# Attention kernel with two passes per head: projections and output products gathered in one gap of the unit, the first block's weighing moved to the next gap

## Chip, core and metric

One core of a Trainium2 chip runs the kernel. The metric is the device time of one execution in microseconds, the median of several. Before the change it is 2521.51 us, the median of three runs between 2519.04 and 2525.44.

## The reference, cut to what matters

The input `x` is 32 x 512 tokens x 256 channels (16 heads of 16). For each of the 32 batches:

```
qk = x @ W_attn + b_attn ; q, k = halves of qk ; v = x          (heads of 16 channels)
y  = causal_softmax(q k^T / 4) v
e  = v[1:] - y[:-1] ; k2 = x[:-1] @ W_k2 + b_k2 ; q2 = q[1:]
y2 = causal_softmax(q2 k2^T / 4) e, shifted by one token (first row zero)
x  = layernorm(x + (y + y2) @ W_proj + 2 b_proj)
```

Then a mixture of 8 experts (top 2) is added and a second layernorm follows. The routing table has 512 rows, so that the experts add to batch 0 alone; for the other batches the kernel folds the two layernorms into one.

## The kernel before

The program is unrolled by hand over a clock of slots. A **unit** is one attention pass over one group of four heads of one batch. There are 8 units in a batch: places 0 to 3 are the first attention, places 4 to 7 the second. A unit has ten slots, and every engine's program is written in the same order of slots. "(3, 6)" is slot 6 of place 3. The letters below are used in the whole text.

TensorE (PE) fills in each slot a PSUM bank of transposed scores (`score_t`, L651) of the present unit for the exponentials, and beside it, in the other half of the array's rows, a bank of plain scores (`score`, L662) of the unit five units ahead, for the row maxima. There are three banks of each kind. These products are gathered in four **runs**: R0 (slots 0, 1, 2), R3 (slots 3, 4), R5 (slots 5, 6, 7) and R8 (slots 8, 9). All other work of PE lies in the four gaps behind the runs:

- gap 1, behind R0: **W123**, the weighing of key blocks 1, 3 and 2 of the previous unit (`weigh`, L612), which adds into `out_t`. At places 3 and 7 a transpose of the maxima follows, **N** (L717).
- gap 2, behind R3: **H** (L677), four transposes of `heads_t`, which ScalarE has copied from `out_t` (L536). At places 1 and 2, **Y** follows (L730), four transposes of `y_sum`. It waits for the last additions into `y_sum` on GpSimd (L476).
- gap 3, behind R5: half a projected tile, three matmuls (**P**, L703), or a quarter of the output projection (**J**, L744), then **W0**, the weighing of block 0, which opens `out_t` anew (L758).
- gap 4, behind R8: the other half of the P tile, or the next quarter of J.

Six places of a batch (7, 0, 1, 2, 4, 5) have a P tile, for the batch ahead; places 3 and 6 have J. P, J, N and Y all write the one PSUM bank `misc`.

ScalarE (ACT) takes an exponential of each `score_t` bank in order of slots (L518). When a P tile is complete it copies `misc` to `part_f` (L528); at (0, 7), (0, 9), (1, 1), (1, 3) it applies the first layernorm to a finished batch (L275), the first time after waiting for `shift` (L263) from GpSimd.

VectorE (DVE) takes the row maxima of each `score` bank (L860) and, behind slot 4, normalises the heads of the previous unit (L891, L897). At (4, 0) and (7, 0) it adds the output projection to `resid` (L907), and at (5, 2) it copies the values of the next batch.

GpSimd (POOL) zeroes the masked half of the exponentials behind every second slot (L429), splits `part_f` into high and low parts three slots behind the copy (`part_h` L449, `part_l` L451), adds in slot 0 the result of the second attention (L476) or makes its values (L483), and adds the doubled bias to `resid` (L437). SP issues the DMAs that stack the split parts, five slots behind the copy, and at (2, 2) loads `resid`, after the previous output has been written.

`PIECES` sets where a P tile ends, and through `piece_ending` also where ACT, POOL and SP do their parts of it:

```
PIECES = {(7, 9): ("k", 0, 0), (0, 9): ("q", 0, 1), (1, 9): ("k", 1, 2), (2, 9): ("q", 1, 3),
          (4, 9): ("k2", 0, 4), (5, 9): ("k2", 1, 5)}
```

Of the kernel before, what the change touches and what calls it, by code (L numbers as in the profile page):

```python
# [45 lines left out]
TRIANGLES = [(512, 2, 1), (512, 2, 1), (512, 2, 2), (512, 2, 2), (256, 4, 1)]  # L46


PIECES = {(7, 9): ("k", 0, 0), (0, 9): ("q", 0, 1), (1, 9): ("k", 1, 2), (2, 9): ("q", 1, 3),
          (4, 9): ("k2", 0, 4), (5, 9): ("k2", 1, 5)}  # L50
N_PIECES = len(PIECES)
RING, KEY_DEPTH, MAX_DEPTH, JUNK = 6, 3, 3, 2

# [7 lines left out]
def piece_ending(place, slot, ahead, batches):  # L61

    if (place, slot) not in PIECES:
        return None
    kind, hf, turn = PIECES[place, slot]
    b = ahead + (2 if place == UNITS - 1 else 1)
    return (kind, hf, b, N_PIECES * b + turn) if 0 <= b < batches else None


def build_layer(nc, x, x_turned, w_attn, b_qk, w_k2, w_proj, b_proj,  # L70
                router_indices, routing_weights, w_up, b_up, w_down, b_down, out):
    batches, tokens, width = x.shape
    blocks = tokens // P
    halves = width // P
# [6 lines left out]
    end = UNITS * batches  # L81
# [4 lines left out]
    with ctx:  # L86
# [6 lines left out]
        def sem(name):  # L93
# [55 lines left out]
        s_weights, s_rows, s_next, s_resid, s_out = (sem(f"s_{n}") for n in ("weights", "rows", "next", "resid", "out"))  # L149
# [4 lines left out]
        s_const, s_ones, s_bias, s_wsplit = (sem(f"s_{n}") for n in ("const", "ones", "bias", "wsplit"))  # L154

        s_key, s_qry, s_pv, s_turned, s_piece, s_yt_pe, s_proj, s_neg_pe = (
            sem(f"s_{n}") for n in ("key", "qry", "pv", "turned", "piece", "yt_pe", "proj", "neg_pe"))

        s_exp, s_heads, s_full, s_yt, s_negh, s_rstd, s_apply = (
            sem(f"s_{n}") for n in ("exp", "heads", "full", "yt", "negh", "rstd", "apply"))  # L160

        s_max, s_negl, s_value1, s_floor, s_rden, s_normal, s_attended, s_stats, s_aggr = (
            sem(f"s_{n}") for n in ("max", "negl", "value1", "floor", "rden", "normal", "attended", "stats", "aggr"))

        s_mask, s_split, s_xsplit, s_value2, s_added, s_biased, s_ln = (
            sem(f"s_{n}") for n in ("mask", "split", "xsplit", "value2", "added", "biased", "ln"))
# [8 lines left out]
        WEIGHTS = 5 * 16  # L175
# [226 lines left out]
        def _(e):  # L402
# [16 lines left out]
            for time in times:  # L419
                unit, slot = divmod(time, SLOTS)  # L420
                place, ahead = unit % UNITS, unit // UNITS


                if 0 <= unit < end and slot % 2:
                    pair = time // 2
# [3 lines left out]
                    e.affine_select(out=view, in_=view, compare_op=ALU.is_ge, fill=0.0, base=-unit_parts(unit)[1],  # L429
                                    pattern=[[0, runs], [0, cut], [1, P]], channel_multiplier=-1).then_inc(s_mask, 1)  # L430

                if (place, slot) == (3, 2) and 0 <= ahead - 1 < batches:
                    wide = bass.AP(bias2[:, :].tensor, bias2[:, :].offset, [list(bias2[:, :].ap[0]), [0, blocks], [1, width]])
                    if ahead == 1:
                        e.wait_ge(s_bias, 1)
                    e.wait_ge(s_resid, 16 * ahead)
                    e.tensor_tensor(resid[:, :, :], resid[:, :, :], wide, ALU.add).then_inc(s_biased, 1)  # L437
# [3 lines left out]
                piece = piece_ending(ended // SLOTS % UNITS, ended % SLOTS, ended // SLOTS // UNITS, batches)  # L441
                if piece:
                    n, i = piece[3], piece[3] % 2
# [10 lines left out]
                for c in range(halves):  # L454
                    b = ahead + 2
# [11 lines left out]
                done = unit - 2  # L467
                if slot == 0 and 0 <= done < end:
                    b, a, g = unit_parts(done)
# [17 lines left out]
                b = ahead - 2  # L487
# [8 lines left out]
                if made and made[2] == 1:  # L496
                    n = halves * made[0] + made[1]
# [100 lines left out]
        def _(e):  # L598
# [17 lines left out]
            for time in times:  # L616
                unit, slot = divmod(time, SLOTS)
                place, ahead = unit % UNITS, unit // UNITS
# [3 lines left out]
                for at in RUNS.get(slot, ()):  # L622
                    now = SLOTS * unit + at
                    here, later = 0 <= unit < end, 0 <= unit + LEAD < end
                    if here:
                        b, a, g = unit_parts(unit)
# [6 lines left out]
                    if later:  # L633
                        b, a, g = unit_parts(unit + LEAD)
                        number = now + SLOTS * LEAD
                        if at == 0 and g % (GROUPS // halves) == 0:
                            hf = g * halves // GROUPS
                            e.wait_ge(s_stack["q", hf], 16 * TERMS * SIDES * (b + 1))
                            e.wait_ge(s_stack["k2" if a else "k", hf], 16 * TERMS * SIDES * (b + 1))
                        if number >= MAX_DEPTH:  # L640
                            u, n = divmod(number - MAX_DEPTH, SLOTS)
                            e.wait_ge(s_max, MAX_BEFORE[SLOTS] * u + MAX_BEFORE[n + 1])
                    for i in range(2):
                        if here and i < len(KEY_BANKS[at]):
                            b, a, g = unit_parts(unit)
                            h, kb, col = KEY_BANKS[at][i]
                            pair, side = divmod(GROUP * g + h, SIDES)
                            rows = slice(SIDE * side, SIDE * side + SCORE_ROWS + MAX_PARTS * (a + 1))
                            keys = (stack_k2 if a else stack_k)[b % 2]
                            n = tokens - P * kb  # L650
                            done = e.matmul(score_t[now % KEY_DEPTH][:, col:col + n], keys[rows, pair, kb * P:(kb + 1) * P],  # L651
                                            stack_q[b % 2][rows, pair, kb * P:tokens], start=True, stop=True)
# [25 lines left out]
                    done.then_inc(s_turned, 1)  # L678


                for c in range(halves):
                    piece = piece_ending(place, slot + 2 * (1 - c), ahead, batches)
                    if piece:
                        kind, hf, b, n = piece
                        if c == 0:
                            if n == 0:
                                e.wait_ge(s_weights, WEIGHTS)
                                e.wait_ge(s_wsplit, 4)
                            if n % N_PIECES == 0:
                                e.wait_ge(s_xsplit, 2 * halves * (b + 1))  # L690
                            if n:
                                e.wait_ge(s_full, n)
                            if place == 1 and ahead >= 1:
                                e.wait_ge(s_yt, halves * ahead - 1)
                            if place == 2 and ahead >= 1:
                                e.wait_ge(s_yt, halves * ahead)
                            if place == 4 and ahead >= 1:
                                e.wait_ge(s_attended, 2 * ahead - 1)
                            if place == 7 and ahead + 1 >= 0:
                                e.wait_ge(s_negl, 2 * ahead + 3)  # L700
                        for i, (pw, px) in enumerate(zip(PARTS_K, PARTS_Q)):
                            w = wk2[pw][:, c, hf, :] if kind == "k2" else wq[pw][:, c, hf + (0 if kind == "q" else halves), :]
                            done = e.matmul(misc[:, :], w, x_t[px][:, c, :], start=(c == 0 and i == 0),  # L703
                                            stop=(c == halves - 1 and i == TERMS - 1))
                        if c == halves - 1:
                            done.then_inc(s_piece, 1)

                for a, b in ((0, ahead + 1), (1, ahead)):
                    if (place, slot) == ((7, 2), (3, 2))[a] and 0 <= b < batches:
# [10 lines left out]
                b = ahead - 1  # L720
                if 0 <= b < batches:
                    for hf in range(halves):
                        if (place, slot) == ((1, 4), (2, 4))[hf]:
                            e.wait_ge(s_full, min(N_PIECES * (b + 2) + 2 + hf, N_PIECES * batches))
                            if hf == 0:
                                e.wait_ge(s_added, GROUPS * (b + 1))
                            else:
                                e.wait_ge(s_yt, halves * b + 1)
                            for t in range(blocks):
                                done = e.transpose(misc[:, t * P:(t + 1) * P], y_sum[b % 2][:, t, hf * P:(hf + 1) * P], ident[:, :])  # L730
                            done.then_inc(s_yt_pe, 1)
                    for pair in range(2):
                        for j in range(2):
                            if (place, slot) == ((3, 6)[pair], (7, 9)[j]):
                                t = 2 * pair + j
                                if j == 0:
                                    e.wait_ge(s_yt, halves * (b + 1))
                                    e.wait_ge(s_full, min(N_PIECES * (b + 2) + (6 if pair else 4), N_PIECES * batches))
                                    if pair:
                                        e.wait_ge(s_attended, 2 * b + 1)  # L740
                                    elif ahead < batches:
                                        e.wait_ge(s_negl, 2 * ahead + 2)
                                for c in range(halves):
                                    done = e.matmul(misc[:, j * width:(j + 1) * width], y_t[:, c, t * P:(t + 1) * P], wp[:, c, :],  # L744
                                                    start=(c == 0), stop=(c == halves - 1))
                                if j:
                                    done.then_inc(s_proj, 1)


                if slot == 7 and 0 <= unit < end:  # L750
                    b, a, g = unit_parts(unit)
                    if a:
                        e.wait_ge(s_value2, GROUPS * b + g + 1)
                    elif g == 0:
                        e.wait_ge(s_value1, b + 1)
                    if unit:
                        e.wait_ge(s_normal, unit)
                    weigh(unit, 0, 0, tokens, start=True)  # L758
# [256 lines left out]
```

## Time and profile before

| | |
|---|---|
| median of 3 runs | 2521.51 us (2519.04 to 2525.44) |
| the profiled execution's own time | 2529.61 us |
| its span (first to last instruction) | 2527.9 us |
| PE busy | 2387.1 us, 94% |
| VectorE busy | 2128.2 us, 84% |
| ScalarE busy | 1759.7 us, 70% |
| GpSimd busy | 1509.2 us, 60% |
| mean granted TensorE clock | 0.981 |

In a row of a timeline the first number is the start in microseconds from the span's start and the second the time from there to the end of the last instruction merged into the row. Matmuls overlap, so what a stretch of PE costs is read from start to start. The bracket at the end of a row is idle time of that engine before it and what ended it. "PEld" is the load of weights.

### The profile page before, as it was taken

Reading aid. Unit: us, or ns where it says so; the run is one execution under the profiler, and the core shown is the slowest. Engines: PE = TensorE matmul, PEld = TensorE weight load, DVE = VectorE, ACT = ScalarE, POOL = GpSimd, SP = SyncE. Lnnn points to the kernel's source line nnn. Section 1 sums busy time; section 2 is a strip of 40 time slices with the busy share of each in tenths; the row PEclk is TensorE's granted clock in tenths of the full one; section 3 lists DMA queues with packets and bytes.
Section 4 is the critical chain, followed back from the end, with each engine's and each line's share of the span. In section 5 each row is a group of like instructions: output and inputs, shape, how many; then the busy total and the mean of one; then the engine's idle time right before and its main releaser. Section 6 shows DMA issues by size and latency. Waiting matters only on the chain.

```text
span 2527.9 us, 64943 instructions
## 1 busy us (share of the span) xinstructions
PE 2387.1 (94%) x19670; PEld 1307.0 (52%) x19670; DVE 2128.2 (84%) x9273; ACT 1759.7 (70%) x3388; POOL 1509.2 (60%) x2342
## 2 busy tenths in 40 slices
PE   2999999999999999999999999999999999999996
PEld 1555555555555555555555555555555555555454
DVE  2889888888898888888988888889888888898655
ACT  0377777777777767777777777777777777777652
POOL 2356666666666656666666666666666666665432
PEclk8699999999999999999999999999999999999998
DMA  5555565565555656555555565555555655455111
GB/s 94 95 92 96 87 108 108 107 118 106 101 100 98 105 103 112 107 100 102 101 97 112 106 117 107 99 99 102 101 109 106 120 107 99 99 101 93 54 62 47
DMA packets 187781, 251.22 MB, mean 99 GB/s; under 512 B 26768, under 2 KB 103192, under 8 KB 187416
## 3 DMA queue, kind: packets, MB, share of 16 engines
q1 hardware_dynamic: 187440, 247.07, 52.8%
q8 instruction: 166, 2.72, 0.6%
q14 instruction: 175, 1.43, 0.2%
HBM read 74.60 MB, written 16.78 MB: 36 GB/s over the span
## 4 chain that ended last, share of the span: by engine, by line
PE 67%; ACT 11%; POOL 8%; issue 8%; DVE 4%; SPq 1%; DMA 1%; ACTq 0%; POOLq 0%; DVEq 0%
PE out_t L612 20%; PE score_t L651 17%; PE misc L703 11%; PE score L662 7%; PE misc L744 5%; ACT heads_t L536 4%; ACT prob L518 4%; PE out_t L677 4%; POOL prob L429 3%; DVE junk L860 2%; POOL part_l L451 2%; PE score L803 1%; PE misc L730 1%; ACT part_f L528 1%; POOL y_sum L476 1%
## 5 line engine op out<-in xcount | busy, mean ns | idle before, releaser
L860 DVE CUSTOM_DVE_ANT_0 junk<-score,mask_rows 128x384 bf16<-128x384 f32 (+3 forms) x3584 | 1688.2, 515 | 275.5 <-PE score L662 241.5
L518 ACT ACTIVATE prob<-score_t 128x512 f32<-128x512 f32 x2560 | 1369.6, 600 | 456.2 <-PE score_t L651 455.3
L429 POOL TENSOR_SCALAR_AFFINE_SELECT prob<-prob 128x512 f32<-128x512 f32 (+1 forms) x1280 | 715.0, 562 | 831.9 <-ACT prob L518 831.5
L651 PE MATMUL score_t<-stack_q,stack_k 50*128 50x128 f32 (+5 forms) x4096 | 997.2, 360 | 21.4 <-DVE max_cols L860 2.4
L662 PE MATMUL score<-stack_k,stack_q 48*128 48x512 f32 (+3 forms) x4096 | 989.2, 348 | 12.4 <-DMA stack_q<-part_l 10.7
L651 PEld LDWEIGHTS score_t<-stack_q,stack_k 50*128 50x128 f32 (+1 forms) x4096 | 611.1, 186 | 572.9 <-ACT prob L518 295.0
L612 PE MATMUL out_t<-prob,value 128*17 128x512 f32 (+3 forms) x8192 | 673.4, 439 | 5.7 <-POOL prob L429 5.5
L662 PEld LDWEIGHTS score<-stack_k,stack_q 48*128 48x128 f32 x4096 | 616.3, 188 | 33.8 <-DVE max_cols L860 12.4
L860 DVE DVE_READ_ACCUMULATOR2_ANT max_cols<- 128x1 f32 x4096 | 339.4, 83 | 0.0
L612 PEld LDWEIGHTS out_t<-prob,value 128*17 128x17 f32 x8192 | 188.3, 97 | 283.0 <-issue 217.8
L451 POOL TENSOR_TENSOR part_l<-part_f,part_h 128x512 fp32r<-128x512 f32 x192 | 255.0, 1328 | 16.2
L536 ACT ACTIVATE heads_t<-out_t,sum_floor 128x512 f32<-128x512 f32 x256 | 176.9, 691 | 86.8 <-PE out_t L612 86.8
L677 PE MATMUL out_t<-ident,heads_t 128*128 128x128 f32 x1024 | 167.7, 286 | 41.3 <-ACT heads_t L536 28.2
L528 ACT ACTIVATE part_f<-misc,bias_qk 128x512 f32<-128x512 f32 x192 | 132.1, 688 | 82.1 <-PE misc L703 82.0
L703 PE MATMUL misc<-x_t_h,wq_h 128*128 128x512 f32 x256 | 129.9, 507 | 36.0 <-DVE wk_l L841 33.7
L677 PEld LDWEIGHTS out_t<-ident,heads_t 128*128 128x128 f32 x1024 | 107.4, 141 | 102.5 <-ACT heads_t L536 102.2
L449 POOL CAST part_h<-part_f 128x512 fp32r<-128x512 f32 x192 | 117.5, 612 | 61.8 <-ACT part_f L528 50.9
L744 PE MATMUL misc<-wp,y_t 128*128 128x256 f32 x512 | 146.1, 409 | 0.0
L860 DVE CUSTOM_DVE_ANT_0 junk<-score,mask_first 128x128 bf16<-128x128 f32 x512 | 146.1, 285 | 0.0
L275 ACT ACTIVATE resid<-resid,shift,rstd 128x256 f32<-128x256 f32 x124 | 75.9, 615 | 41.5 <-POOL shift L263 41.5
L703 PE MATMUL misc<-x_t_l,wq_h 128*128 128x512 f32 x256 | 103.3, 403 | 0.0
L744 PEld LDWEIGHTS misc<-wp,y_t 128*128 128x128 f32 x512 | 88.6, 192 | 26.3 <-issue 10.6
(98 smaller groups left out, 1718.4 us busy)
## 6 DMA issues: line engine op xcount, KB each, us to landing
stack_k<-part_h SPq DMA_DIRECT2D x512, 128.0 KB, 5.0
stack_k<-part_l SPq DMA_DIRECT2D x256, 128.0 KB, 4.6
stack_q<-part_h SPq DMA_DIRECT2D x256, 128.0 KB, 4.2
x_full<-x_turned SPq DMA_DIRECT2D x32, 512.0 KB, 10.4
x_in<-L_attn_x SPq DMA_DIRECT2D x32, 512.0 KB, 14.5
stack_q<-part_l SPq DMA_DIRECT2D x128, 128.0 KB, 5.1
resid<-L_attn_x SPq DMA_DIRECT2D x32, 512.0 KB, 5.6
layer_out<-resid SPq DMA_DIRECT2D x31, 512.0 KB, 6.1
```

The source lines that it names most:

```text
L429: e.affine_select(out=view, in_=view, compare_op=ALU.is_ge, fill=0.0, base=-unit_parts(unit)[1], pattern=[[0, runs], [0, cut], [1, P]], ch ...
L451: e.tensor_tensor(part_l[i][:, :], part_f[i][:, :], part_h[i][:, :].bitcast(F32), ALU.subtract).then_inc(s_split, 1)
L518: e.activation(prob[pair % RING][:, slot % 2 * 512:slot % 2 * 512 + 512], score_t[time % KEY_DEPTH][:, :], ACT.Exp, scale=1.0 / np.sqrt(HE ...
L528: e.activation(part_f[n % 2][:, :], misc[:, :], ACT.Identity, bias=bias_qk[:, column:column + 1]).then_inc(s_full, 1)
L536: e.activation(heads_t[:, :], out_t[:, :], ACT.Identity, bias=sum_floor[:, 0:1]).then_inc(s_heads, 1)
L612: done = e.matmul(out_t[32 * h:32 * h + HEAD_DIM + 1, first:first + count], value[:, kb, GROUP * g + h, :], prob[pair % RING][:, at:at + c ...
L651: done = e.matmul(score_t[now % KEY_DEPTH][:, col:col + n], keys[rows, pair, kb * P:(kb + 1) * P], stack_q[b % 2][rows, pair, kb * P:token ...
L662: done = e.matmul(score[number % MAX_DEPTH][:, col:col + n], stack_q[b % 2][rows, pair, qb * P:(qb + 1) * P], keys[rows, pair, 0:n], start ...
L677: done = e.transpose(out_t[:, t * P:(t + 1) * P], heads_t[:, t * P:(t + 1) * P], ident[:, :])
L703: done = e.matmul(misc[:, :], w, x_t[px][:, c, :], start=(c == 0 and i == 0), stop=(c == halves - 1 and i == TERMS - 1))
L744: done = e.matmul(misc[:, j * width:(j + 1) * width], y_t[:, c, t * P:(t + 1) * P], wp[:, c, :], start=(c == 0), stop=(c == halves - 1))
L860: e.tensor_tensor_reduce(junk[count % JUNK][:, 0:n], score[number % MAX_DEPTH][:, col:col + n], mask, 1.0, -3e38, ALU.add, ALU.max, max_co ...
```

## The change

The P tile is made whole at slot 7: both halves of its contraction, six matmuls, one behind the other. The entries of `PIECES` move from slot 9 to slot 7, and with them ACT's copy, POOL's split and SP's DMAs move two slots forward. Each pair of output quarters J is made whole at slot 7 too. W0 moves from slot 7 to slot 9, behind R8. POOL's addition of the doubled bias moves from (3, 2) to (3, 6).

```diff
-PIECES = {(7, 9): ("k", 0, 0), (0, 9): ("q", 0, 1), (1, 9): ("k", 1, 2), (2, 9): ("q", 1, 3),
-          (4, 9): ("k2", 0, 4), (5, 9): ("k2", 1, 5)}
+PIECES = {(7, 7): ("k", 0, 0), (0, 7): ("q", 0, 1), (1, 7): ("k", 1, 2), (2, 7): ("q", 1, 3),
+          (4, 7): ("k2", 0, 4), (5, 7): ("k2", 1, 5)}
...
-                if (place, slot) == (3, 2) and 0 <= ahead - 1 < batches:
+                if (place, slot) == (3, 6) and 0 <= ahead - 1 < batches:
...
-                for c in range(halves):
-                    piece = piece_ending(place, slot + 2 * (1 - c), ahead, batches)
-                    if piece:
-                        kind, hf, b, n = piece
-                        if c == 0:
...
+                piece = piece_ending(place, slot, ahead, batches)
+                if piece:
+                    kind, hf, b, n = piece
...
+                    for c in range(halves):
                         for i, (pw, px) in enumerate(zip(PARTS_K, PARTS_Q)):
...
-                        if c == halves - 1:
-                            done.then_inc(s_piece, 1)
+                    done.then_inc(s_piece, 1)
...
-                            if (place, slot) == ((3, 6)[pair], (7, 9)[j]):
+                            if (place, slot) == ((3, 6)[pair], 7):
...
-                if slot == 7 and 0 <= unit < end:
+                if slot == 9 and 0 <= unit < end:
                     b, a, g = unit_parts(unit)
```

The waits of a P tile are the same ones as before, asked for once at its start.

## Rows read from the trace of the kernel before

**Rows 1.** Part 1 of the page: busy time of each engine.

```profile
PE 2387.1 (94%) x19670; PEld 1307.0 (52%) x19670; DVE 2128.2 (84%) x9273; ACT 1759.7 (70%) x3388; POOL 1509.2 (60%) x2342
```

**Rows 2.** Busy time by window; clock and DMA share at the end.

```profile
1209.90:1282.00 72.10, 70.17 (x610) 38.48 (x606) 63.99 (x286) 53.80 (x104) 46.27 (x73) 1.00 0.57 105
```

**Rows 3.** Who waited for whom: us in total, times, longest.

```profile
PE out_t L677 <- ACT heads_t L536: 28.2, 30, 1.0
...
POOL resid L437 <- DMA resid<-L_attn_x: 9.4, 7, 2.4
```

**Rows 4.** Timeline of PE, place 2: from gap 3 to W123.

```profile
1208.24 0.50 PE L703 MATMUL misc<-x_t_h,wq_h 128*128 128x512 f32 x1
1208.59 0.39 PE L703 MATMUL misc<-x_t_h,wq_l 128*128 128x512 f32 x1
1208.82 0.40 PE L703 MATMUL misc<-x_t_l,wq_h 128*128 128x512 f32 x1
1209.14 1.05 PE L612 MATMUL out_t<-prob,value 128*17 128x512 f32 x8
1210.13 0.38 PE L651 MATMUL score_t<-stack_q,stack_k 50*128 50x256 f32 x1
...
1210.79 0.50 PE L703 MATMUL misc<-x_t_h,wq_h 128*128 128x512 f32 x1
...
1211.69 0.50 PE L651 MATMUL score_t<-stack_q,stack_k 50*128 50x512 f32 x1
...
1212.74 1.49 PE L612 MATMUL out_t<-prob,value 128*17 128x384 f32 x24
```

**Rows 5.** The same timeline, place 3: from gap 3 to W123.

```profile
1217.14 1.13 PE L744 MATMUL misc<-wp,y_t 128*128 128x256 f32 x4
1218.20 1.48 PE L612 MATMUL out_t<-prob,value 128*17 128x512 f32 x8
1219.61 0.38 PE L651 MATMUL score_t<-stack_q,stack_k 50*128 50x256 f32 x1
...
1220.28 1.13 PE L744 MATMUL misc<-wp,y_t 128*128 128x256 f32 x4
1221.34 0.49 PE L651 MATMUL score_t<-stack_q,stack_k 52*128 52x512 f32 x1
...
1222.23 1.49 PE L612 MATMUL out_t<-prob,value 128*17 128x384 f32 x24
```

**Rows 6.** Timeline of POOL, place 3.

```profile
1213.93 2.37 POOL L437 TENSOR_TENSOR resid<-resid,bias 128x1024 f32<-128x1024 f32 x1
...
1218.16 1.61 POOL L429 TENSOR_SCALAR_AFFINE_SELECT prob<-prob 128x256 f32<-128x256 f32 x3
```

**Rows 7.** Timelines of ACT, of PE and of POOL, places 0 and 1.

```profile
1189.19 0.51 PE L703 MATMUL misc<-x_t_h,wq_h 128*128 128x512 f32 x1
...
1192.08 0.60 ACT L275 ACTIVATE resid<-resid,shift,rstd 128x256 f32<-128x256 f32 x1 [1.37 <-POOL shift L263]
...
1193.55 0.69 ACT L528 ACTIVATE part_f<-misc,bias_qk 128x512 f32<-128x512 f32 x1
1194.12 0.60 ACT L275 ACTIVATE resid<-resid,shift,rstd 128x256 f32<-128x256 f32 x1
...
1196.53 0.72 ACT L536 ACTIVATE heads_t<-out_t,sum_floor 128x512 f32<-128x512 f32 x1
...
1197.31 0.66 PE L677 MATMUL out_t<-ident,heads_t 128*128 128x128 f32 x4 [0.96 <-ACT heads_t L536]
...
1194.38 0.74 POOL L476 TENSOR_TENSOR y_sum<-y_sum,y_second 128x256 f32<-128x256 f32 x1
```

**Rows 8.** Timelines of DVE, rows with idle before them: places 7, 4, 6.

```profile
1175.75 0.69 DVE L860 CUSTOM_DVE_ANT_0 junk<-score,mask_rows 128x512 bf16<-128x512 f32 x1 [0.26 <-PE score L662]
...
1228.77 0.43 DVE L860 CUSTOM_DVE_ANT_0 junk<-score,mask_rows 128x256 bf16<-128x256 f32 x1 [0.32 <-PE score L662]
1241.53 0.69 DVE L860 CUSTOM_DVE_ANT_0 junk<-score,mask_rows 128x512 bf16<-128x512 f32 x1 [0.54 <-PE score L662]
```

More of the change, by code:

```diff
@@ L678, in _ @@
                     done.then_inc(s_turned, 1)
-                for c in range(halves):
-                    piece = piece_ending(place, slot + 2 * (1 - c), ahead, batches)
-                    if piece:
-                        kind, hf, b, n = piece
-                        if c == 0:
[L686 to L700, printed above, removed]
+                piece = piece_ending(place, slot, ahead, batches)
+                if piece:
+                    kind, hf, b, n = piece
+                    if n == 0:
+                        e.wait_ge(s_weights, WEIGHTS)
+                        e.wait_ge(s_wsplit, 4)
+                    if n % N_PIECES == 0:
+                        e.wait_ge(s_xsplit, 2 * halves * (b + 1))
+                    if n:
+                        e.wait_ge(s_full, n)
+                    if place == 1 and ahead >= 1:
+                        e.wait_ge(s_yt, halves * ahead - 1)
+                    if place == 2 and ahead >= 1:
+                        e.wait_ge(s_yt, halves * ahead)
+                    if place == 4 and ahead >= 1:
+                        e.wait_ge(s_attended, 2 * ahead - 1)
+                    if place == 7 and ahead + 1 >= 0:
+                        e.wait_ge(s_negl, 2 * ahead + 3)
+                    for c in range(halves):
                         for i, (pw, px) in enumerate(zip(PARTS_K, PARTS_Q)):
```

## The prediction

> **What bounds the kernel.** I read the busy times first: PE 2387.1 of 2527.9 us [rows 1]. A busy PE proves little, since its matmuls overlap, so I took one batch, eight units from W123 of one place 2 to the next, in the window view: 72.1 us, of which PE is busy 70.17, DVE 63.99, ACT 53.80 and POOL 46.27, at a granted clock of 1.00, the 2.4 GHz level [rows 2]. So PE's own order sets the period, DVE follows 11% behind, and no gain below some 64 us per batch is possible. Next come the waits that reach PE [rows 3]. Last I read PE's timeline from start to start, for what each piece costs in its place [rows 4, 5], and the engines that PE waits for [rows 6 to 8].
>
> **What a boundary costs.** In gap 3 of place 2 the P matmuls start at 1208.24, 1208.59 and 1208.82 and W0 at 1209.14 [rows 4]. The steps are 0.35, 0.23 and 0.32 us: within P one matmul follows another in 0.23, the step into P costs 0.11 more and the step out 0.10. The second half in gap 4 costs 1210.79 to 1211.69 = 0.90 again. So three matmuls cost 0.90, and six in a row should cost 0.90 + 3 x 0.23 = 1.59 in place of 1.80. One entry and one exit go, **0.21 us per P unit**. J costs 1.06 twice (1217.14 to 1218.20, 1220.28 to 1221.34) [rows 5]. Its inner steps are merged in the row; I take the same entry and exit, 0.20 saved. W0 costs 0.99 behind P and pays its way in and out wherever it stands; R8 costs 0.66 ahead of P and I take that ahead of W0. TensorE: Matmul & The Clock Gate in the Trainium skill ("Back-to-back issue gap") gives about N/2.4 + 2.5 ns from start to start, 216 ns for 512 columns, with no charge for what stands before. By it a P half would take 0.65 us, the boundary would be free and the merge worth nothing; the 0.90 us of [rows 4] speaks against it, and it is rival 3.
>
> **The change part by part**, against this batch of 72.1 us.
>
> - *Merging P* takes 0.21 in each of six units, if nothing else binds. It makes gap 3 1.59 in place of 1.89 (P + W0) and gap 4 0.98 in place of 0.90. R8 follows R5 0.30 sooner, R0 follows R8 0.08 later.
> - *R0 ahead of W123.* Behind P, R0 takes 1.05 us [rows 4], behind J 0.89 [rows 5]. The longer gap 4 (1.06) is what I hold responsible: the third product of R0 waits for VectorE's maxima of R8's last bank, and behind the short gap it is just late, which costs 0.16 with the refill. With W0 in gap 4 the maxima have 0.08 more. Worth between 0 and 0.16; I take 0.11, at places 1 and 2.
> - *VectorE's slack* in front of R8's first maxima is 0.32 us at place 4 [rows 8], which is just what R8 comes sooner. So places 0, 2 and 4 keep their 0.21. At place 5 there is none: from 1228.77 to 1241.53 no row of [rows 8] shows VectorE idle for long. Here VectorE is the bound, and place 5 gains **0**; the R0 gain of place 4 is lost in the same chain. Place 7 is nearly the same, VectorE working on from 1175.75 [rows 8]; between 0.06 and 0.28, I take 0.17.
> - *The bias addition.* It holds GpSimd 2.37 us from 1213.93, the split follows, and the masks come at 1218.16 in a row of three [rows 6]. W0 of place 3 needs them and takes 1218.20 to 1219.61 = 1.41 in place of 0.99 [rows 4, 5]: **0.42 us** per batch, all of it a wait. After, the split stands in slot 0, the addition behind the mask of slot 5, and W0 comes 2 us later: the wait goes. The addition then holds POOL about 1217.5 to 1219.9. The mask of slot 7 is done at 1220.5. R0 of place 4, at 1221.34 before [rows 5], comes 0.62 sooner, at 1220.7; W123 behind it needs that mask at 1221.6, and VectorE needs the sum behind its first maxima, at about 1221.9. Both are covered, by 1.1 us and more; without the cover either costs what it is late.
> - *The wait for the resid load.* 9.4 us in 7 batches [rows 3] ended in W0 through the same masks. Four slots on is some 3.5 us, more than its longest 2.4: all 9.4 go.
> - *ACT at places 0 and 1.* ACT idles 1.37 us until 1192.08 for `shift`, then runs without a pause: exponentials, `part_f` at 1193.55, the norm, more exponentials, `heads_t` at 1196.53; H starts at 1197.31, having idled 0.96 [rows 7]. Over all batches H waits 28.2 us for `heads_t` in 30 long waits [rows 3], 0.9 each. P of place 0 starts at 1189.19 [rows 7]; after, its sixth matmul starts 0.35 + 4 x 0.23 = 1.27 later and ends 0.4 behind, at 1190.86, so `part_f` fills the idle stretch and is out of the way: the chain from 1193.55 to `heads_t` is shorter by one copy, 1194.12 - 1193.55 = **0.57 us** by the starts on ACT. What stands ahead of 1193.55 is tied to `shift`, so place 0 itself gains nothing: R0 of place 1 waits for the same exponentials at the same time.
> - *GpSimd's slot 0.* The split takes 1.86 us (from the bias addition's end at 1216.30 to 1218.16 [rows 6]) and now stands ahead of the last `y_sum` addition, which was made at 1194.38 [rows 7]. The mask of slot 9 ends by about 1194.1, the split by 1195.95, the addition (0.74) by 1196.7. H comes at 1197.31 - 0.57 = 1196.74, and Y, behind its four transposes (about 0.5), needs the sum at 1197.2. Covered by 0.5 us; if late, place 1 pays it.
> - *Other queues.* SP stacks the parts two slots sooner; the units that read them are over a unit away, and the load of `resid` ahead of one of them on SP delays nothing that PE waits for. The exponential of slot 2 waits for W0 of the unit before to free its probabilities: W0 now ends as R0 begins, and that exponential cannot start before R0's third product. No cost, with about 1 us of cover. W0's other waits (values, the normalised heads) get later users, never sooner ones. All DMAs are the same in number.
>
> **The sum per batch:** place 1: 0.57 + 0.21 + 0.11 = 0.89; place 2: 0.21 + 0.11 = 0.32; place 3: 0.42 + 0.20 = 0.62; place 4: 0.21; place 5: 0; place 6: 0.20; place 7: 0.17; place 0: 0. Together 2.41 us, so 69.7 in place of 72.1. Over the 31 steps between 32 batches 74.7 us, and the resid waits 9.4: 84.1. The start and the expert stage at the end I leave as they are. The profiled execution took 2529.6 us (1.7 around its span), so 2445.5; the median of the runs was 8.1 lower than it, so I predict **2438 us** as the median, -3.3%.
>
> **Bounds.** Most: all eight merges pay in full (another 0.6 per batch), R0 gains 0.16 and at place 4 too (another 0.25): 3.26 x 31 + 9.4 = 110, 2411. Least of this mechanism: half the boundary at only four units (0.4), no R0 gain, the bias wait 0.42, half of the 0.57: 1.1 x 31 + 9 = 43, 2478.
>
> **The rivals.**
>
> 1. *As worked out*, 2425 to 2455: chance 0.60.
> 2. *VectorE takes the gain.* It would be busy 64 of 69.7 us, and the margins at places 0, 2 and 4 are within 0.03 us of zero. If its maxima of R8 are late, R0's third product waits, and the merges at those places are given back there. What is left is the two waits (0.42 + 0.57), the J units and place 1, about 1.6 per batch: 2521.5 - 50 - 9 = 2463. For it: place 5, already so. Against: the 0.32 and more of idle. 0.15.
> 3. *The boundary is not saved but moved*, R8 into W0 costing what P gave up. Only the waits go: (0.42 + 0.57) x 31 + 9.4 = 40, 2481. Against it: J and P show the same entry and exit whatever stands before. 0.08.
> 4. *More than that*, 2411 to 2420, if places 5 and 7 gain too because VectorE's chain was bound through PE after all. 0.08.
> 5. *Slower:* POOL's slot 0. The split ahead of the `y_sum` addition makes Y late, and behind Y stand R5, the P tile and with it ACT's next copies. The cover is 0.5 us by my working. It decides from 0.5 + 2.4 = 2.9 us of lateness on, each further 0.3 us costing 9 us; with a lateness of 3.4, 2537. Nothing in the rows is as late; but a ring of waits through POOL, which is at 64% in this stretch, can settle at another beat. 0.05.
> 6. *No change*, the gains all returned as waits of other engines, within 0.3% of 2521.5: 0.04.
>
> A difference under 0.3% can't be told from none here. Faster: 0.60 + 0.15 + 0.08 + 0.08 = 0.91; same 0.04; slower 0.05. The range that leaves out 2 in 10: 2416 to 2478. The first case alone: 2425 to 2455.
>
> **What the profile after would show.** Six P matmuls from entry to the next start at R8 in 1.59 us, and J in 1.93. W0 at place 3 at 0.99. R0 at places 2 and 3 at 0.89 to 0.94. H at place 1 with an idle of 0.4 or less. No `resid` wait on POOL above 1 us in total. VectorE with hardly any idle ahead of R8, and the batch at 69.7 us. I am wrong if R0 grows at places 1, 3 and 5 (VectorE, rival 2), if R8 or W0 grows (rival 3), or if Y waits for L476 (rival 5).

## The result: slower, 2601.9 us, and the profile after

The changed kernel takes 2601.9 us (median of four runs, 2596.8 to 2609.8) against 2520.3 for the kernel before; the ratio is 1.0329, interval 1.0297 to 1.036. The forecast was 2438, faster. The profiled execution took 2599.5 us, with a mean granted clock of 0.962 in place of 0.981.

What was forecast of TensorE's order came about. Six P matmuls at place 7, in the timeline of PE of the changed kernel:

```profile
1211.39 0.51 PE L702 MATMUL misc<-x_t_h,wq_h 128*128 128x512 f32 x1
1211.73 0.39 PE L702 MATMUL misc<-x_t_h,wq_l 128*128 128x512 f32 x1
1211.96 0.40 PE L702 MATMUL misc<-x_t_l,wq_h 128*128 128x512 f32 x1
1212.19 0.40 PE L702 MATMUL misc<-x_t_h,wq_h 128*128 128x512 f32 x1
1212.43 0.39 PE L702 MATMUL misc<-x_t_h,wq_l 128*128 128x512 f32 x1
1212.66 0.39 PE L702 MATMUL misc<-x_t_l,wq_h 128*128 128x512 f32 x1
1212.98 0.38 PE L651 MATMUL score_t<-stack_q,stack_k 52*128 52x256 f32 x1
```

From 1211.39 to R8 at 1212.98 is 1.59 us, where the halves took 0.90 each [rows 4]. All J products in one took 1.92 in the median in place of 2 x 1.06 [rows 5]. The loss is at one place of the batch. The timeline of PE from J of place 3 on:

```profile
1246.74 1.99 PE L742 MATMUL misc<-wp,y_t 128*128 128x256 f32 x8
1248.67 0.38 PE L651 MATMUL score_t<-stack_q,stack_k 50*128 50x256 f32 x1
...
1249.34 1.05 PE L612 MATMUL out_t<-prob,value 128*17 128x512 f32 x8
1253.98 0.50 PE L651 MATMUL score_t<-stack_q,stack_k 52*128 52x512 f32 x1 [3.59 <-DMA stack_q<-neg_l]
...
1254.87 2.63 PE L612 MATMUL out_t<-prob,value 128*17 128x384 f32 x24
1257.44 0.79 PE L651 MATMUL score_t<-stack_q,stack_k 52*128 52x512 f32 x1
```

W0 ends near 1250.3, and R0 of place 4 waits until 1253.98 for the row maxima of the second attention, which SP lays into the rows of `stack_q` that R0 reads. Behind the pause W123 takes 2.57 us from start to start in place of 1.42. The windows (busy PE, PEld, DVE, ACT, POOL, then granted clock, DMA share, GB/s) say why:

```profile
1249.00:1252.00 3.00, 1.39 (x16) 0.34 (x12) 1.47 (x8) 1.09 (x2) 2.47 (x4) 1.00 0.85 117
1252.00:1255.00 3.00, 1.02 (x10) 0.62 (x14) 0.45 (x1) 0.42 (x1) 0.00 (x0) 1.00 0.05 7
1255.00:1258.00 3.00, 3.00 (x26) 1.29 (x21) 2.07 (x7) 1.60 (x4) 0.42 (x1) 0.51 0.00 0
1258.00:1261.00 3.00, 3.00 (x25) 2.28 (x22) 2.66 (x13) 2.57 (x6) 0.96 (x2) 0.92 0.00 0
```

Behind the 3.59 us of idle TensorE is granted 0.51 of its clock from 1255 to 1258, the 1.2 GHz level, then 0.92 in the next 3 us. In the medians over 27 batches W0 with the wait is 4.36 us (0.98 without), then R0 1.25 (0.96), W123 2.68 (1.42), R3 1.06 (0.88): 3.4 us of waiting and 1.7 us of slow clock, 5.1 per batch. The eight units add to 74.7 us, where 69.7 was forecast. The clock did not fall in every batch: in 4 of the 31 with such a wait (2.5 to 3.0 us idle) W123 kept its 1.42.

SP's timeline names the cause. First the kernel before, then the changed one, both at place 3 (N, which starts the road of the maxima, is at 1214.16 and 1243.76):

```profile
1215.88 1.18 SPq L367 DMA_DIRECT2D stack_q<-neg_h  x2
1217.11 2.41 SPq L367 DMA_DIRECT2D stack_q<-neg_l  x2
1219.62 2.52 SPq L356 DMA_DIRECT2D stack_q<-part_h  x4
1222.17 1.24 SPq L356 DMA_DIRECT2D stack_q<-part_l  x2
```

```profile
1244.19 3.75 SPq L356 DMA_DIRECT2D stack_q<-part_h  x4
1247.99 1.25 SPq L356 DMA_DIRECT2D stack_q<-part_l  x2
1249.34 1.18 SPq L367 DMA_DIRECT2D stack_q<-neg_h  x2
1250.56 1.22 SPq L367 DMA_DIRECT2D stack_q<-neg_l  x2
```

Before, the maxima went out as soon as VectorE had them and the six DMAs of the P tile of place 2 behind them. Now the tile, two slots sooner, stands at (3, 2) and the maxima at (3, 3), behind five microseconds of issuing. VectorE makes the low halves (`neg_l`) from 1245.18 to 1245.46; SP issues the high halves from 1249.34 and the low ones from 1250.56.

Two things make the maxima late. From N to the start of the last issue it was 3.58 us in the median of the batches and is now 6.37. From there to its landing it was 2.15 us and is now 3.2 (2.15 to 5.7), so the last row lands 9.9 us behind N in place of 5.9. The second part goes with the tile's own transfers: behind the issues, from 1250 to 1252, the DMA share is 0.81, in the kernel before, from 1219 to 1221.5, it was 0.22. No run here parts the two; both come and go with the order.

The cover was small already before: the last landing came 1.4 us ahead of R0 in the median, and 0.2 us in the closest batches. This row of the kernel before, the weight load of R0 of place 4, was in the trace and not used in the forecast. It names that landing as the last of its waits, as 4 of 32 batches do, and is from a batch in which the landing was only 0.2 us ahead.

```profile
1221.34 0.18 PEld L651 LDWEIGHTS score_t<-stack_q,stack_k 52*128 52x128 f32 x1 [0.33 <-DMA stack_q<-neg_l]
```

### The profile page after: what moved, and what is told of

The parts are those of the page before. It is cut to its first block, busy times and chain, and to the rows that moved or that the text cites. A ratio compares the mean times of both kernels' runs of the same rounds, so it can differ in the third digit from the quotient of the medians.

```text
span 2597.8 us, 64943 instructions
## 1 busy us (share of the span) xinstructions
PE 2365.0 (91%) x19670; PEld 1341.8 (52%) x19670; DVE 2124.4 (82%) x9273; ACT 1765.8 (68%) x3388; POOL 1503.3 (58%) x2342
## 4 chain that ended last, share of the span: by engine, by line
PE 53%; ACT 11%; issue 9%; SPq 8%; DVE 7%; POOL 6%; DMA 5%; POOLq 0%; DVEq 0%; ACTq 0%
PE out_t L612 17%; PE score_t L651 14%; PE misc L702 7%; PE score L662 6%; SPq L356 5%; DMA stack_q<-neg_l 5%; ACT prob L518 5%; DVE junk L858 4%; ACT heads_t L536 4%; PE out_t L677 3%; PE misc L742 3%; POOL prob L429 2%; SPq L367 2%; POOL part_l L451 2%; PE score L801 2%
## 5 line engine op out<-in xcount | busy, mean ns | idle before, releaser
L651 PE MATMUL score_t<-stack_q,stack_k 50*128 50x128 f32 (+5 forms) x4096 | 1007.4, 364 | 137.4 <-DMA stack_q<-neg_l 108.6
L662 PE MATMUL score<-stack_k,stack_q 48*128 48x512 f32 (+3 forms) x4096 | 1000.5, 352 | 11.2 <-DMA stack_q<-part_l 8.1
L651 PEld LDWEIGHTS score_t<-stack_q,stack_k 50*128 50x128 f32 (+1 forms) x4096 | 622.2, 189 | 688.8 <-ACT prob L518 282.0
L612 PE MATMUL out_t<-prob,value 128*17 128x512 f32 (+3 forms) x8192 | 685.3, 455 | 0.0
L662 PEld LDWEIGHTS score<-stack_k,stack_q 48*128 48x128 f32 x4096 | 628.3, 191 | 34.8 <-DVE max_cols L858 12.4
L451 POOL TENSOR_TENSOR part_l<-part_f,part_h 128x512 fp32r<-128x512 f32 x192 | 245.3, 1278 | 16.3
L702 PE MATMUL misc<-x_t_h,wq_h 128*128 128x512 f32 x256 | 117.9, 460 | 36.2 <-DVE wk_l L839 33.9
L742 PE MATMUL misc<-wp,y_t 128*128 128x256 f32 x512 | 127.2, 392 | 0.0
L483 POOL TENSOR_TENSOR value<-x_next,y_sum 128x256 f32<-128x256 f32 x128 | 107.3, 838 | 0.0
L702 PE MATMUL misc<-x_t_h,wq_l 128*128 128x512 f32 x256 | 103.5, 404 | 0.0
```

The lines of the kernel that those rows point to most:

```text
L451: e.tensor_tensor(part_l[i][:, :], part_f[i][:, :], part_h[i][:, :].bitcast(F32), ALU.subtract).then_inc(s_split, 1)
L612: done = e.matmul(out_t[32 * h:32 * h + HEAD_DIM + 1, first:first + count], value[:, kb, GROUP * g + h, :], prob[pair % RING][:, at:at + c ...
L662: done = e.matmul(score[number % MAX_DEPTH][:, col:col + n], stack_q[b % 2][rows, pair, qb * P:(qb + 1) * P], keys[rows, pair, 0:n], start ...
```

## The experiments

Ratios are against the kernel before on the same chip.

**The maxima first** (`a1_maxima_first`), the changed kernel with one tile's DMAs moved:

```diff
                 ended = time - 5
+                if (ended // SLOTS % UNITS, ended % SLOTS) == (2, 7):
+                    ended = -1000
+                if (place, slot) == (3, 4):
+                    ended = time - 7
```

> The changed kernel, in which SP stacks the P tile of place 2 at (3, 4), behind the four DMAs of the row maxima at (3, 3), in place of (3, 2), ahead of them; nothing else differs. Theory A, SP's order: the changed kernel waits in R0 of place 4 for neg_l only because its DMAs stand behind the six of the tile. Then W0 of place 3 takes about 1.0 us again in place of 4.36, the granted clock stays at 1.00 behind it, the batch comes to 69.7 us and the time to 2435 to 2455. Rival B, the road of the maxima is too long by itself for the denser order (they come 4.9 us ahead of R0, and two of the DMAs may land slowly): W0 of place 3 stays above 2 us and the time between 2480 and 2560. Rival C, the loss lies in the fallen clock, which another pause of PE brings about as well: a wait of some 3 us turns up at another place and the time stays above 2560.

Measured: 2448.4 us (2446.0 to 2458.4), ratio 0.9708 (0.9689 to 0.9727). SP and PE at place 3:

```profile
1248.32 2.47 SPq L371 DMA_DIRECT2D stack_q<-neg_h  x2
1250.84 1.22 SPq L371 DMA_DIRECT2D stack_q<-neg_l  x2
1252.16 2.51 SPq L360 DMA_DIRECT2D stack_q<-part_h  x4
```

```profile
1252.17 1.05 PE L616 MATMUL out_t<-prob,value 128*17 128x512 f32 x8
1253.67 0.50 PE L655 MATMUL score_t<-stack_q,stack_k 52*128 52x512 f32 x1 [0.44 <-DMA stack_q<-neg_l]
```

This is one of 8 batches in which a short wait is left (here 0.44 us; two issues of `neg_h` took 2.47). In the median W0 of place 3 takes 0.98, in the mean 1.18. The batch is 69.7 us, in the window view of eight units (the profiled execution, at 2458, was the slowest of the four):

```profile
1209.00:1278.70 69.70, 67.67 (x606) 38.88 (x606) 63.29 (x282) 53.47 (x104) 45.52 (x73) 1.00 0.59 108
```

Theory A holds; rivals B and C fall. The order of four small DMAs and one tile's six on SP's queue decides between 2602 and 2448 us.

**All tiles in their old slots on SP** (`a2_sp_as_before`), `ended = time - 7` for every tile:

> The changed kernel with all six P tiles stacked by SP seven slots behind the copy in place of five, that is in the slots in which the kernel before has them. Theory A: only the order of place 2's tile against the maxima counts, so this is within 5 us of the run with that tile alone moved, 2435 to 2455. If the other tiles' earlier stacking matters too (the read of the stacks, or contention with other loads), the two differ by more than 5 us. Rivals B and C: as in that run, above 2480.

Measured: 2450.7 us, ratio 0.9719 (0.9701 to 0.9736), 2 us from the run above. Only place 2's tile counts.

**The old kernel with the order reversed** (`b1_maxima_behind`):

```diff
-                    if (place, slot) == ((7, 3), (3, 3))[a] and 0 <= b < batches:
+                    if (place, slot) == ((7, 3), (3, 4))[a] and 0 <= b < batches:
```

> The kernel before with one edit: SP issues the second attention's maxima at (3, 4), behind the six DMAs of place 2's tile, in place of (3, 3). In the kernel before that tile's split ends at about 1218.2 us on its clock, so the maxima go out at 1222.0 to 1224.5 and land at about 1226.5, where R0 of place 4 wants them at 1221.3. Theory A: R0 of place 4 waits about 5 us per batch, the clock falls behind it to the 1.2 GHz level for some microseconds, and the time comes to 2521 + 31 x (5 + 1.5) = 2700 to 2740. Theory B or C, if SP's order is not what costs: under 2600.

Measured: 2767.9 us in one run. PE and SP at place 3 of this kernel:

```profile
1331.99 2.48 SPq L356 DMA_DIRECT2D stack_q<-part_h  x4
1334.51 1.25 SPq L356 DMA_DIRECT2D stack_q<-part_l  x2
1335.86 1.18 SPq L367 DMA_DIRECT2D stack_q<-neg_h  x2
1337.08 1.22 SPq L367 DMA_DIRECT2D stack_q<-neg_l  x2
```

```profile
1341.22 0.79 PE L651 MATMUL score_t<-stack_q,stack_k 52*128 52x512 f32 x1 [6.06 <-DMA stack_q<-neg_l]
```

PE idles 6.06 us, and the batch grows by 8.4 us (72.1 to 80.5) where 6.5 was expected; the time is outside the 2700 to 2740 expected. The sign and the place are as theory A says; the size was short. The last issue ends near 1338.3 and R0 starts at 1341.2, 2.9 behind it and not 2.0: the last row lands 3.6 us behind the start of its issue in the median, where it took 2.15 in the kernel before. The slow clock costs 2.2 us of the batch and not 1.5. A mere swap of queue order on SP costs the kernel before 248 us.

**The bias addition alone** (`b2_bias_only`), the kernel before with (3, 2) changed to (3, 6) on POOL:

> The kernel before with the addition of the doubled bias at (3, 6) in place of (3, 2), nothing else. By the prediction's term W0 of place 3 falls from 1.40 to 0.98 us and the waits for the resid load (9.4 us) go: 0.42 x 32 + 9.4 = 23 us, 2498. Rival: the masks of slots 7 and 9 then come late behind the addition, W123 of place 4 waits for them and gives back part: 2505 to 2525.

Measured: 2505.0 us, ratio 0.9934 (0.9918 to 0.9951), so 14.4 us, where 23 was expected. W0 of place 3 fell to 0.98 and the batch from 72.1 to 71.7: 0.42 x 32 = 13.4. The 9.4 us of waits for `resid` [rows 3] did not come on top in the medians. Between the two profiled executions they did: 2529.6 and 2504.8 us, 24.8 apart, of which W0 of place 3 makes 22. So those waits belong to the one execution that was profiled. The rival, W123 of place 4 late, is not there: it takes 1.42 in both.

**The bias addition in its old place** (`d2_bias_old`), the run with the maxima first and POOL's addition at (3, 2):

> The run with the maxima ahead (2448 us), with the doubled bias added at (3, 2) again. With W0 at slot 9 the masks that stand behind the addition are wanted 2 us later than in the kernel before. If W0's new place alone covers them, W0 of place 3 stays at 0.98 us in the median and only the late loads of resid, which come to 2.4 us, may show: 2446 to 2456. If the addition's place is what took the wait away, W0 of place 3 is 1.2 us or more: 2458 to 2470.

Measured: 2449.0 us, ratio 0.9726 (0.9713 to 0.974), as without the edit (0.9708). The move is worth 14 us alone and nothing beside W0 at slot 9, whose masks are then wanted 2 us later. The two cures take away the same wait.

**The copy of P late** (`c2_copy_late`), the run with the maxima first, ScalarE copying at `time - 2`:

> The run with the maxima ahead (2448 us), with ScalarE copying each P tile at slot 9 as in the kernel before, though TensorE has made it at slot 7. The prediction's term: at places 0 and 1 the copy stands again in the chain from the norm's shift to heads_t, so R3 with the wait for heads_t at place 1 goes from 1.16 back to about 1.75 us, 0.57 x 31 = 18 us: 2460 to 2470. Rival, the 0.57 came from the earlier end of the P tile or from W0's new place, not from the copy's order on ScalarE: no change at place 1, 2445 to 2452.

Measured: 2460.2 us, ratio 0.9763 (0.9739 to 0.9788), 12 us more than with the early copy. R3 of place 1 with its wait went from 1.16 to 1.74 us, 0.58; R5 of place 5 gave 0.09 back, and the batch went from 69.7 to 70.2. The waits view, first of the run with the maxima first, then of this one:

```profile
ACT resid L275 <- POOL shift L263: 14.8, 30, 1.7
PE out_t L681 <- ACT heads_t L540: 11.6, 31, 0.4
```

```profile
ACT resid L275 <- POOL shift L263: 41.2, 30, 1.7
PE out_t L682 <- ACT heads_t L541: 28.3, 31, 1.0
```

With the copy late ScalarE idles 41.2 us for `shift` again (41.5 in the kernel before), and TensorE waits 28.3 us for `heads_t`, the same as before [rows 3]. The rival falls: the copy's place in ScalarE's order is what gains.

**W0 back in gap 3** (`c3_w0_gap3`), `if slot == 7` in place of `if slot == 9`, with the maxima first:

> The run with the maxima ahead (2448 us), with W0 back at slot 7, behind the whole P tile, so that nothing lies between R8 and R0. TensorE's own work is the same or, a boundary less, up to 0.1 us per unit less. Theory: R0's third product waits for VectorE's maxima of R8, about 2.2 us behind R8's start, and gap 4 is what hides it; without cover R8 and R0 take 2.6 us together in place of 1.6, near 1 us per unit, so 2448 + 31 x 6 to 8 = 2630 to 2700. Rival, VectorE is ahead of TensorE by then and only the sum of TensorE's work counts: 2420 to 2470.

Measured: 2647.1 us, ratio 1.0503 (1.0483 to 1.0524). R8 and R0 take 2.62 us together in every unit but place 7's (2.86), as expected. PE from W0 of place 3:

```profile
1301.59 1.05 PE L616 MATMUL out_t<-prob,value 128*17 128x512 f32 x8
1302.57 0.38 PE L655 MATMUL score_t<-stack_q,stack_k 52*128 52x256 f32 x1
...
1304.06 0.47 PE L655 MATMUL score_t<-stack_q,stack_k 52*128 52x512 f32 x1 [0.52 <-DVE max_cols L862]
1304.75 0.47 PE L655 MATMUL score_t<-stack_q,stack_k 52*128 52x512 f32 x1 [0.19 <-ACT prob L522]
1305.18 1.49 PE L616 MATMUL out_t<-prob,value 128*17 128x384 f32 x24
```

The rival, that only the sum of TensorE's work counts, falls. In this schedule something must lie between R8 and R0 while VectorE takes the maxima.

**The high halves early** (`c1_high_early`) and **the values on GpSimd** (`c4_values_pool`), each on the run with the maxima first, and **both** (`d1_both`):

```diff
-                        e.wait_ge(s_negl, 2 * b + a + 1)
+                        e.wait_ge(s_negh, 2 * b + a + 1)
                         if b >= 2:
                             e.wait_ge(s_key, SLOTS * UNITS * (b - 1))
                         for part, tile in enumerate((neg_h, neg_l)):
+                            if part:
+                                e.wait_ge(s_negl, 2 * b + a + 1)
```

The other edit takes the copy into `value1` out of VectorE's program at (5, 2) and puts the same waits and the same copy into GpSimd's at (5, 6).

> The run with the maxima ahead of place 2's tile (2448 us), and in it SP sends the high halves of the maxima as soon as ScalarE has made them, in place of waiting for the low halves from VectorE, about 0.6 us sooner. In that run W0 of place 3 is 0.98 us in the median but 1.18 in the mean and 2.45 at most, waits for the last landing of the maxima. If the wait is the length of that road, it shortens: mean of W0 at place 3 under 1.08, 2440 to 2447. If it is slow landings beside other loads, whatever the issue time: no difference, 2446 to 2452.

> The run with the maxima ahead (2448 us), with the copy of the next batch's values made by GpSimd behind the mask of slot 5 at place 5 in place of VectorE at (5, 2). If VectorE is the bound at place 5, R5 of place 5 falls from 1.38 to about 1.09 and R0 behind it from 1.12 to 0.96: 0.3 to 0.45 us per batch, 2434 to 2440. If GpSimd's copy makes the masks of slots 7 and 9 late, W123 of place 6 grows by what they are late and it comes to 2448 or more.

> The run with the maxima ahead of place 2's tile, and in it both edits that gained alone: the high halves sent early (2443 us) and the values copied by GpSimd (2443 us). They touch different waits, the landing of the maxima at place 4 and VectorE's load at place 5, so the gains of some 5 us each should add: 2436 to 2440. If the run with GpSimd's copy gained little because its own waits for the maxima at place 4 were longer (mean W0 of place 3 1.24 us), sending early takes those too and it comes to 2432 to 2437. If the two gains were chance between runs, 2441 to 2450.

Measured: 2443.4 us, ratio 0.9696 (0.9672 to 0.972); 2443.1 us, ratio 0.9692 (0.967 to 0.9715); both 2434.1 us, ratio 0.9666 (0.9652 to 0.9679). The two single gains are no larger than their uncertainty, and the copy's 2443 misses the 2434 to 2440 expected; together they stand clear of the run without them. The last issue of the maxima comes 2.87 us behind N in place of 3.58. That this alone gains is not shown: the mean of W0 at place 3 fell from 1.18 to 1.09, but it is 1.05 in `a2_sp_as_before` and 1.03 in `d2_bias_old` too, which send no earlier. The median batch of `d1_both` is 69.2 us in place of 69.7, all of it from places 5 and 0, where the copy acts. With the copy moved alone W0 of place 3 is over 1.02 us in 15 of 32 batches, with both edits in 5, as the expectation's second case has it. With the copy gone from VectorE, R5 of place 5 takes 1.09 us from 1258.96 to 1260.05, where it took 1.39 with the maxima first alone:

```profile
1258.96 0.32 PE L663 MATMUL score_t<-stack_q,stack_k 52*128 52x128 f32 x1
...
1260.05 0.50 PE L714 MATMUL misc<-x_t_h,wk_h 128*128 128x512 f32 x1
```

R0 of place 0 also fell, from 1.36 to 1.12; R0 of place 6 stayed at 1.12, against the expectation. `d1_both` is the fastest version measured, 84 us ahead of the kernel before.

## Why the prediction was wrong

The step that failed is *Other queues*: "SP stacks the parts two slots sooner; the units that read them are over a unit away". I asked who reads the moved DMAs, and not what they are moved ahead of. Slot (3, 4) minus two is (3, 2), and the maxima are at (3, 3). Six issues of about 0.62 us each, and at times slower, stood ahead of four whose reader came 4.9 us behind VectorE's last part. Without the six, the last landing is 4.0 us behind it and 0.8 ahead of R0 (`a1_maxima_first`, in a batch with no slow issue). The six took 2.8 us from the start of the last issue and another 1.1 from its landing. The step was put at "no cost"; it cost 5.1 us per batch, 3.4 of waiting and 1.7 of slow clock, and 154 us in all. None of the rivals had it: the slower one was put on POOL's slot 0, where nothing was late. The chance of 0.05 for slower came from that single place, with two other in-order queues passed over in a sentence.

The rest, read in `a1_maxima_first`, the changed kernel less this one fault:

- *Boundary.* 1.59 and 1.92 us, as worked out (1.59, 1.93). W0 takes 0.98 in its new place and R8 0.67 (0.71 at places 5 and 7): rival 3 falls. Within P the trace has 230 ns from start to start, and 0.1 us more on each side. The Trainium skill, in TensorE: Matmul & The Clock Gate ("Back-to-back issue gap"), has 216 ns for 512 columns as the gap of an isolated matmul, with no charge for the neighbour. In the Trainium skill, TensorEngine Tiling (Array Packing) ("Key Properties") says that a change of tiling mode drains the engine. The trace is nearer to this: the runs use half the array's rows, P all of them. No run here tells a drain from another cost of the change.
- *R0 ahead of W123.* 0.95 to 0.97 at places 2, 3, 4, 5 and 7 (0.94 expected at 2 and 3), a gain of 0.08 behind P where 0.11 was taken. That VectorE's maxima need the cover is what `c3_w0_gap3` shows. R0 of place 1 grew, from 1.51 to 1.62, one of the signs named for rival 2; but the wait in it is for ScalarE's exponentials, and the stretch as a whole grew shorter.
- *Place 5* gained nothing (R5 1.39 and R0 1.12, before 1.34 and 1.05), as forecast, and `c4_values_pool` shows that VectorE's load was the bound of R5 there. What holds R0 behind it is open. From R5 to W123 the stretches that begin at places 5, 7 and 0 became 0.04, 0.08 and 0.08 us shorter, where 0, 0.17 and 0 were forecast.
- *Bias and masks.* 0.42 per batch, the right size. But it was laid to the addition's move; W0's new slot removes it by itself.
- *ACT at places 0 and 1.* R3 with its wait 1.16 us from 1.75, 0.58 where 0.57 was forecast; `c2_copy_late` undoes it.
- *The sum.* 69.7 us per batch was forecast and 69.7 measured. That it fits to 0.1 is in part luck: places 4 and 0 gained 0.14 and 0.08 more than forecast, places 3, 6 and 7 0.06, 0.06 and 0.09 less. The time is 2448 and not 2438 (2445.5 less 8.1 is nearer 2437), because two terms counted one thing. The 9.4 us of `resid` waits belonged to the profiled execution, which was 8.1 us slower than the median, and I subtracted both. `b2_bias_only` gives the bias move 14.4 us in the medians, its 13.4 and no 9.4 more. Without them the same working gives 2447.

## What to carry to other kernels

When a step moves in a schedule, write down for each in-order queue (DMA issuers too) the list of entries that it passes, and for each of them the time from its issue to its reader's need, less what it takes to land, which was longer behind bulk transfers here. A small, late-made transfer with a near reader belongs ahead of bulk transfers whose readers are far. Two cures of one wait are not two gains; and a term taken from one profiled execution must not be subtracted together with that execution's own distance from the median.

## What the runs showed of the hardware

A pause of TensorE can cost more than its length: behind 3.6 us of idle it was granted 0.51 of its clock for 3 us, and over the batches this adds 1.7 us, a third of the loss. In 4 of the 31 pauses (2.5 to 3.0 us) the clock did not fall, and behind one of 2.2 us it did, so that in these traces the length alone does not tell.

Issuing on SP does not scale with the size of a transfer: the 16 KB DMAs of the maxima take about 0.6 us each to issue, as the 128 KB ones do, and some of either size took 1.5 us and more. So six issues are some 3.7 us of issuing ahead of what stands behind them, whatever they carry. Landing is another matter: the same 16 KB landed 2.15 us behind the start of its issue, and 3.2 us (3.6 in `b1_maxima_behind`) behind the six 128 KB transfers.
